# Second gather stage of a graph-transformer kernel: 11 of 782 source tiles fetched row by row from the SyncE queue

## The reference, cut to what matters

```python
src = node_in[edge_src]                    # 100000 rows of 256, gathered from 6250
s0 = src[:, :MUL]
s1 = src[:, MUL:].reshape(-1, MUL, 3)
out0 = alpha * (einsum(s0 * a0, w_00_0) + inv_sqrt3 * einsum(s1, a1, w_11_0))
out1 = alpha * (einsum(s0, w_01_1, a1) + einsum(s1 * a0, w_10_1))
messages = concatenate([out0, out1]) * msg_rad
agg = segment_sum(messages, edge_dst, num_segments=6250)
```

## Time and profile before

| | us |
|---|---|
| median of 3 runs | 2966.12 (2966.08 to 2967.82) |
| the profiled execution, its own time | 2963.22 |
| its span, first to last instruction | 2961.6 |
| TensorE busy in the span | 2613.7 (88%) |
| GpSimd busy | 1789.0 (60%) |
| VectorE busy | 1696.1 (57%) |
| ScalarE busy | 1447.5 (49%) |
| gathers of the second stage, line 2550 | 782, from 1575.2 to 2571.2 us |

### The profile page before, as it was taken

How to read it: one execution, slowest core, us unless ns; L and a number is a source line. 1 busy time by engine, 2 the same in 40 slices (tenths; PEclk the granted TensorE clock), 3 DMA queues, 4 the chain that set the end, 5 groups by cost and what they waited for, 6 DMA issues and landing times. The chain is left out here.

```text
span 2961.6 us, 53196 instructions
## 1 busy us (share of the span) xinstructions
PE 2613.7 (88%) x14911; PEld 2205.2 (74%) x14911; DVE 1696.1 (57%) x5391; ACT 1447.5 (49%) x4052; POOL 1789.0 (60%) x1939
## 2 busy tenths in 40 slices
PE   2999999999888899599994999898888878789998
PEld 1877778889878788488883766666677777678887
DVE  6733324788665567545553656666677767534333
ACT  4122222463222555245656978787667756422222
POOL 5777777777776255446666777777777777500000
PEclk9999999999999999799996999999899989989999
DMA  8464455777675486345555444444466655532222
GB/s 234 118 194 140 142 144 176 233 222 238 214 220 176 154 244 218 117 123 161 163 154 149 132 137 130 140 127 137 124 181 190 181 159 162 150 105 71 78 74 59
DMA packets 292358, 464.33 MB, mean 157 GB/s; under 512 B 89481, under 2 KB 224050, under 8 KB 290988
## 3 DMA queue, kind: packets, MB, share of 16 engines
q1 hardware_dynamic: 210438, 238.37, 27.1%
q0 software_dynamic: 81216, 221.98, 25.8%
q10 hardware_dynamic: 432, 0.79, 0.1%
HBM read 349.16 MB, written 111.83 MB: 156 GB/s over the span
## 5 line engine op out<-in xcount | busy, mean ns | idle before, releaser
L2550 POOL DMA_INDIRECT g_got<-xm_d,idx x782 | 759.1, 971 | 250.6 <-issue 220.9
L883 POOL DMA_INDIRECT g_got<-xn_d,idx x702 | 677.6, 965 | 229.1 <-issue 213.6
L2189 PEld LDWEIGHTS ps<-g_hotw,g_got 128*128 128x128 f32 x3128 | 407.9, 198 | 207.1 <-DMA g_got<-xm_d,idx 164.4
L2189 PE MATMUL ps<-g_hotw,g_got 128*128 128x128 f32 (+11 forms) x3128 | 435.3, 288 | 141.5 <-DMA g_got<-xm_d,idx 134.9
L1282 PEld LDWEIGHTS ps<-g_hot,g_got 128*128 128x128 f32 x2808 | 354.8, 195 | 103.0 <-DMA g_got<-xn_d,idx 74.1
L1282 PE MATMUL ps<-g_hot,g_got 128*128 128x120 f32 (+4 forms) x2808 | 374.5, 280 | 54.9 <-DMA g_got<-xn_d,idx 54.1
L2599 ACT ACTIVATE g_hotw<-g_hot,g_wr 128x16 f32<-128x16 f32 (+8 forms) x1308 | 299.4, 309 | 34.5 <-DVE g_hot L590 34.3
L1482 POOL TENSOR_TENSOR p_ln_rs<-p_ln_pre,neg_half 125x2 f32<-125x2 f32 x50 | 35.2, 703 | 460.3 <-DVE p_ln_pre L1477 460.3
L2104 POOL DMA_INDIRECT z_d<-p_yj,p_to x108 | 128.0, 1185 | 140.8 <-DVE p_to L2137 121.5
L3021 ACT ACTIVATE p_hid<-ps,p_b 128x250 f32<-128x250 f32 x200 | 82.8, 466 | 251.5 <-PE ps L2982 251.5
L2081 PE MATMUL ps<-gin_hid,p_wj 128*128 128x256 f32 x864 | 197.6, 382 | 0.9 <-DVE p_wj L2127 0.8
(11 more groups left out here) (389 smaller groups left out, 4854.3 us busy)
## 6 DMA issues: line engine op xcount, KB each, us to landing
h_d<-gin_hid SPq DMA_DIRECT2D x23, 1000.0 KB
gin_hid<-h_d SPq DMA_DIRECT2D x23, 1000.0 KB
job_in<-jobs_d SPq DMA_DIRECT2D x54, 258.0 KB, 3.0
g_got<-xm_d,idx POOLq DMA_INDIRECT x782
g_got<-xn_d,idx POOLq DMA_INDIRECT x702
p_z<-z_d SPq DMA_DIRECT2D x50, 224.0 KB
q_d<-g_qo SPq DMA_DIRECT2D x25, 250.0 KB, 2.8
g_xa<-xn_d SPq DMA_DIRECT2D x50, 125.0 KB
```

Of the source, the lines that this page charges most:

```text
L883: landed.start(e.indirect_dma_start(got[:, k % (2 * GB), :], None, xn_d[0:N, :], bass.IndirectOffsetOnAxis(ap=idx[:, HT + k:HT + k + 1], a ...
L2189: mm = e.matmul(to, rows[j][:, c * P:(c + 1) * P], hotw[:, j, c * w:4 * w].unsqueeze(1).broadcast_to([P, r, n]), start=(j == 0), stop=(j = ...
L2550: landed.start(e.indirect_dma_start(got[:, 2 * (g % GB) + j, :], None, xm_d[0:N, :], bass.IndirectOffsetOnAxis(ap=idx[:, 2 * g + j:2 * g + ...
```

## The change

The second tile of 11 groups is not gathered by POOL. SP copies its 128 rows one at a time. The groups are `SIDE[n]` = 37 + 32 n, that is 37, 69, and so on to 357. The rows of one such tile are spread over 32 steps, 4 rows per step (`PACE`), from step 4 + 32 n on; they stand last in SP's list at their step. The row number comes from a table of source indices: `load_ids` copies 128 of them into partition 32 of the tensor that held only `base` before, and each 16 of them are read into registers with one `reg_load`. Seven of the tiles land in slots of `f3T`, four in slots of `wq`, both unused at those steps. SP waits for the index load, for the `sums` that last read the same slot (for n from 3 to 6), and once, at n = 7, for the product that last reads `wq`. TensorE waits in `sums` of a `SIDE` group for one gather instead of two on `landed` and for 128 rows on the semaphore `far`.

```diff
+            PACE, TURNS, FAR0, READ = 4, P // 4, 4, 16
+            SIDE = [FAR0 + TURNS * (n + 1) + 6 - LEAD - FIRST for n in range(11)]
...
+            OLD = next(n for n in range(len(SIDE)) if FAR0 + TURNS * n > MIX[0] + 4)
...
+            def far(n):
+                return spots[:, n % 3 * D:(n % 3 + 1) * D] if n < OLD else wq[:, n % IC, :]
+
+            def far_last(n):
+                return (n - 3 if n < OLD else n - IC if n - IC >= OLD else -1)
...
+                    def fetch(i):
+                        n, q = divmod(i, TURNS)
+                        if q == 0:
+                            e.wait_ge(s_ids, 16 * (n + 1))
+                            if far_last(n) >= 0:
+                                summed.wait(e, SIDE[far_last(n)], "sums")
+                            if n == OLD:
+                                e.wait_ge(s_m, 2)
+                        for p in range(PACE * q, PACE * (q + 1)):
+                            if p % READ == 0:
+                                e.reg_load(numbers, ids[0:1, n % 3 * P + p:n % 3 * P + p + READ])
+                            row = e.snap(numbers[p % READ], min_val=0, max_val=N - 1)
+                            e.dma_start(far(n)[p:p + 1, :], xm_d[ds(row, 1), :]).then_inc(s_far[n % 2], 16)
...
-                        for j in range(2):
+                        for j in range(1 if g in SIDE else 2):
...
-                        landed.wait(e, g % GB, g // GB)
+                        e.wait_ge(landed.sems[g % GB], 16 * arrivals[g])
+                        if g in SIDE:
+                            n = SIDE.index(g)
+                            e.wait_ge(s_far[n % 2], 16 * P * (n // 2 + 1))
```

More of the change, by code:

```diff
@@ L2368, in gps_kernel @@
             rel = ph.sb("rel", [P, NG, 2])
-            base = ph.sb("base", [1, NG], I32)
+            table = ph.sb("base", [33, NG], I32)
+            base, ids = table[0:1, :], table[32:33, :]
             wr = ph.sb("wr", [P, 2, P, 4])
@@ L2409, in gps_kernel @@
                 ph.sem(n) for n in ("in", "w", "c", "p", "z", "m", "f", "wb", "w2r", "wz", "wd"))
-            landed = ph.landing("got", GB, 2)
+            landed = ph.landing("got", GB)
+            s_ids, s_far = ph.sem("ids"), [ph.sem(f"far{u}") for u in range(2)]
             ready = ph.steps("ready", "hot", "hotw")
@@ L2449, in gps_kernel @@
             GROUPS = every(FIRST, 1, NG)
+            PACE, TURNS, FAR0, READ = 4, P // 4, 4, 16
+            SIDE = [FAR0 + TURNS * (n + 1) + 6 - LEAD - FIRST for n in range(11)]
+            assert (2 * SIDE[-1] + 2) * P <= E and SIDE[-1] + LEAD < NG
+            arrivals = [sum(1 if k in SIDE else 2 for k in range(g % GB, g + 1, GB)) for g in range(NG)]
             UNITS = [(n, v) for n in range(1, NCH) for v in range(NV)]
@@ L2466, in gps_kernel, with tile_rows @@
             LAST_STEP = P9[-1] + 26
+            OLD = next(n for n in range(len(SIDE)) if FAR0 + TURNS * n > MIX[0] + 4)
+            assert FIRST + SIDE[OLD - 1] + LEAD < F3[0] + 3
+            spots = f3T[:, :, :, :].rearrange("p u c n -> p (u c n)")
+            def far(n):
+                return spots[:, n % 3 * D:(n % 3 + 1) * D] if n < OLD else wq[:, n % IC, :]
+            def far_last(n):
+                return (n - 3 if n < OLD else n - IC if n - IC >= OLD else -1)
+            def tile_rows(g):
+                return [far(SIDE.index(g)) if j and g in SIDE else got[:, 2 * (g % GB) + j, :] for j in range(2)]
             XT, KB, V, DOTS = 4, 3, 5, 6
@@ L2541, in store_f3T, with load_ids @@
                         t_out.start(e.dma_start(f3T_d[i], f3T[:, i % FR, :, :].rearrange("p c n -> p (c n)")), i % FR)
-                    timeline(LAST_STEP, (CHUNKS[:-1], [(lambda i: load_emb(i + 2), 2)]), (KV, [(store_kT, 4), (load_kv, 0)]), ([FIRST], [(load_rest, 0)]),
-                             (P9, [(load, 0), (store_x3, 6)]), (F3, [(store_f3, 1), (store_f3T, 6)]))
+                    def load_ids(n):
+                        at = (2 * SIDE[n] + 1) * P
+                        e.dma_start(ids[:, n % 3 * P:(n % 3 + 1) * P], A["src"][at:at + P].rearrange("(a n) -> a n", a=1)).then_inc(s_ids, 16)
+                    numbers = [e.alloc_register(f"g2_row{k}") for k in range(READ)]
+                    def fetch(i):
[11 more added lines that the diff above has]
+                            e.dma_start(far(n)[p:p + 1, :], xm_d[ds(row, 1), :]).then_inc(s_far[n % 2], 16)
+                    timeline(LAST_STEP, ([max(FIRST, FAR0 + TURNS * n - 20) for n in range(len(SIDE))], [(load_ids, 0)]),
+                             (CHUNKS[:-1], [(lambda i: load_emb(i + 2), 2)]), (KV, [(store_kT, 4), (load_kv, 0)]), ([FIRST], [(load_rest, 0)]),
+                             (P9, [(load, 0), (store_x3, 6)]), (F3, [(store_f3, 1), (store_f3T, 6)]),
+                             (every(FAR0, 1, TURNS * len(SIDE)), [(fetch, 0)]))
                 @block.gpsimd
@@ L2782, in sums @@
                         added.wait(e, BEFORE[g], "add")
-                        summed.done(edge_sums(e, bank_of(g)[0], [got[:, 2 * (g % GB) + j, :] for j in range(2)],
+                        summed.done(edge_sums(e, bank_of(g)[0], tile_rows(g),
                                               hotw[:, g % HR, :, :], WINS[g], bank_of(g)[1]), "sums")
```

## The result

| | before | changed |
|---|---|---|
| median, us | 2966.97 (4 runs, 2966.08 to 2970.89) | 2980.9 (4 runs, 2978.69 to 2983.73) |
| profiled execution, us; span | 2963.22; 2961.6 | 2978.69; 2977.1 |

The ratio is 1.0047, 95% interval 1.0035 to 1.0058: 14 us slower where 14 us faster was forecast.

A forecast was written before the change was run, and what follows sets the result against it. POOL's gathers were taken to bound the stage: eleven fewer at 1.276 us each take 14.0 us off 2966.1, with SP's added work and the DMA engines costing nothing, giving 2952.1 us; range 2949 to 2967.

The forecast's parts named there:

- What bounds the stage: POOL's gathers, one after the other at 1.276 us each, set the stage's length; eleven fewer give 14.0 us less.
- The fetch: On SP, a one-row copy was put at 0.46 us, four per step, from a lone row copy at line 2951.
- The register load: On SP, 0.53 us per 16 words, 0.13 us per step, more words taken as no dearer.
- What SP has to give: SP's present waits were taken as free time: 2.27 us per step in `KV`, 2.00 in `P9`, against 1.97 needed.
- What is absorbed: SP's lag was to be hidden by 15 us of load lead and 25 us of slots, so SP's share was 0.
- Rival 1: SP becomes the bound through dearer fetches, deciding at 0.52 us each; 2969 us at 0.55, 3037 at 0.60; chance 0.18.
- Rivals 2 and 3: TensorE or VectorE takes the gain, 2961.4 us, chance 0.10; one full DMA engine delays rows or inputs, 2952 to 2975, 0.06.
- the estimate for the DMA engines: Fetches at 61 ns per packet, 0.24 us per step, at most 10% of one engine's time; the sum does not move.

## Why the prediction was wrong

- **What bounds the stage** held. One gather after the other on POOL, and where SP fits, each tile taken off gives its 1.276 us: the gathers' stretch fell from 996 us to 981 with eleven tiles and one register load (982 by the sum), to 987.5 with seven (987).
- **The fetch** held: about 0.43 us against 0.46, from the single row copy of the earlier trace rows.
- **The register load** is the step that failed, 43 of the 48 us that SP took too long in `P9`. The prediction said that "more words do not show as dearer", from one word at 532 ns on SP and four at 345 ns on another engine. Two numbers from two engines say nothing of a slope. Measured on SP it is 0.57 us for 4 words, 1.23 for 16 and 2.11 for 32, 0.055 us per word from 4 on; and 1.3 to 3.0 us for 16 where it stands behind a store of a whole node tile. In the sum for `P9` it was 0.13 us per step and was 0.47: with 1.72 of fetches 2.19 us, where 1.97 was forecast.
- **What SP has to give** was a little less than forecast: 326 - 82 = 244 us in the 128 steps, 1.91 us per step and not 2.00, and 11 us of it went to waits that stayed. In the 270 us of the earlier trace rows SP's own DMAs, counted from start to start, take 66 us, so 204 and not 211.8 us were free.
- **What is absorbed** was too generous: 15 us of lead of the loads and 25 us of slots. With the measured 48 us of lag the prediction's own formula gives 48 - 40 = 8 us of loss and a time of 2960, not 2981; with the register load alone put right the lag would be 39 us, within the 40, and the sum would still have said 2952. So the register load alone does not turn the sign: own DMAs and waits added to the lag, the pace to keep was 319 us and not 326, and less than 40 us was absorbed. The runs give what is absorbed as one number. SP's excess over 319 us was 55 us in the changed kernel, 55 with the `P9` tiles only (2151.4 to 2525.3) and 41 with the loads moved. Against what the tiles taken off should give, the losses were 28 us (1.0047 - 0.9953), 30 (1.0084 - 0.9983) and 11 (0.9991 - 0.9953). In `KV`, excess 44 and 261 us gave 14 and 228. Each time 25 to 33 us are absorbed, in both parts. One reason is in the profiles above. The lead of the loads was 15 us, as forecast, but it fell only to about 4 us, from 2184 us on, and stayed there, near the time that a DMA of this size takes to land; so 11 us of it could be used. The slots did give what was forecast. A tile has 4 matmuls, so tiles gathered and matmuls done give how far TensorE is behind; until 2375 us, before and with the change:

```profile
1570.00:2375.00 805.00, 332.36 (x2488) 314.06 (x2488) 609.14 (x627) 0.94 0.53 149
```
```profile
1570.00:2375.00 805.00, 319.32 (x2372) 303.56 (x2372) 599.44 (x618) 0.93 0.52 147
```

That is (627 - 622) / 2 = 2.5 groups and (618 - 593) / 2 = 12.5 groups, with POOL held at 13. The 11 and 25 us make 36; why the runs show up to 11 us less stays open.
- **Rival 1** was the right mechanism, with its order of events: loads late, TensorE idle before `P9` products, pauses of POOL up to 4 us. It had a chance of 0.18. Its trigger was put on the price of the fetch; it came by the load beside it. And it had SP behind in both parts, while in `KV` SP kept 28 us of waits. The forecast had SP "exactly" full in `P9` and still had a chance of 0.64: a term known from two unlike rows should have moved the chance and the upper end of the range.
- **Rivals 2 and 3** did not appear: with one register load TensorE took the full gain, and with the 1408 one-row DMAs in place the gathers took 981 us against the 982 of the sum. A copy came out as two packets, where the estimate for the DMA engines had one: SP's queue has 2838 more, two for each of the 1408 rows and 11 index copies, and its share went from 27.1 to 27.2%.

```profile
q1 hardware_dynamic: 213276, 239.82, 27.2%
```

## What to carry to other kernels

An engine that mostly waits has free time per step, and work can be moved to it only up to that: add every instruction of the moved work, the loads of addresses too, and leave room for terms that no row shows in their real size and place. The versions that kept their gain left SP waiting 5% of the time beside `KV` (25 of 500 us, seven tiles) and 9% beside `P9` (23 of 270 us, ten tiles); the changed kernel left 4% there (11 of 270). When a transfer queue falls behind, look for the delay not at the moved work but at the ordinary loads that stand behind it. Take the moved work down in steps; here seven tiles gave 0.36% and eleven lost 0.47%. Look also whether an edit is still in the program that ran: a register load whose result nobody needs was gone in two of these experiments. And run on more than one chip: what gained 0.4% on one lost 2.7% on another.

## What the runs showed of the hardware

- A register load on SP costs by the word: medians of 0.57 us for 4 words, 1.23 for 16, and 2.11 for 32 (this one only on a chip where the kernel before takes 3427 us). Two words took 0.73 us, more than four, also at the same place in the list (0.64 against 0.49); this was not expected and has no test.
- 16 words took 1.3 to 3.0 us directly behind a store of 125 or 128 rows (20 loads of the changed kernel), 1.24 us in the median behind a DMA of one row.
- One-row DMAs of 1 KB with a register address run at one per 0.43 us on SP, 228 ns of it the DMA instruction. With 1408 of them beside the gathers, the gathers kept their 946 ns each.
- The same program took 2966 to 2972 us on some chips and 3423 to 3427 us on two others.
